# Three groups of heads on the first batch, conditioning of the second batch over nine units, one weight group loaded twice, and a new order of the last blocks

## The reference, cut to what matters

```python
def cond(r, k, v, w, u, temb):          # forward and backward decaying scans along T
    tf = sigmoid(sum(temb)); decay = exp(-exp(w)) * (0.5 + 0.5*tf)
    ek = exp(min(k, 30)); ekv = ek * v
    nf, df = scan(ekv), scan(ek)        # a = a*decay + x
    nb, db = scan_reverse(ekv), scan_reverse(ek)
    euk = exp(min(u + k, 30))
    return sigmoid(r) * (nf+nb-ekv+euk*v) / max(df+db-ek+euk, 1e-8) * (0.8+0.2*tf)
x = x + attention(cond(x, fside, fside, w1, u1, temb))   # 16 causal heads, W_K/Q/V/O
y = cond(x, fside, fside, w2, u2, temb)
x = x + sum_of_top2_of_8_experts(y) # each expert 256x256 plus bias, softmaxed gates
```

## Time and profile before

| | |
|---|---|
| median of 3 runs | 381.71 us (381.62 to 381.79) |
| the profiled execution | 381.94 us |
| its span | 380.1 us |
| TensorE busy | 351.5 us, 92% of the span |
| VectorE busy | 317.6 us, 84% |
| ScalarE busy | 255.8 us, 67% |
| GpSimd busy | 212.3 us, 56% |
| mean granted TensorE clock | 0.982 of full |

### The profile page before, as it was taken

How to read it: one execution, slowest core, us unless ns; L and a number is a source line. 1 busy time by engine, 2 the same in 40 slices (tenths; PEclk the granted TensorE clock), 3 DMA queues, 4 the chain that set the end, 5 groups by cost and what they waited for, 6 DMA issues and landing times.

```text
span 380.1 us, 7412 instructions
## 1 busy us (share of the span) xinstructions
PE 351.5 (92%) x2404; PEld 323.6 (85%) x2404; DVE 317.6 (84%) x883; ACT 255.8 (67%) x685; POOL 212.3 (56%) x223
## 2 busy tenths in 40 slices
PE   0897789999999999999999999999999998798997
PEld 0686679999999999899999999999999886685785
DVE  4979899999898988999899989998676747476576
ACT  5678888788778878877987889787877643210100
POOL 1865677864647669767857966886744341210000
PEclk9998899999999999999999999999999999898999
DMA  5660130100000000130100041000000000000000
GB/s 170 243 252 3 55 112 0 58 3 0 2 0 3 2 0 2 55 114 2 55 2 1 3 166 57 3 1 2 0 3 2 1 0 2 0 29 1 28 29 28
DMA packets 4597, 14.12 MB, mean 37 GB/s; under 512 B 840, under 2 KB 1872, under 8 KB 3920
## 3 DMA queue, kind: packets, MB, share of 16 engines
q1 hardware_dynamic: 4336, 13.65, 10.6%
q10 hardware_dynamic: 224, 0.01, 0.0%
HBM read 12.60 MB, written 1.05 MB: 36 GB/s over the span
## 4 chain that ended last, share of the span: by engine, by line
PE 67%; DVE 25%; issue 4%; ACT 3%; DMA 1%; DVEq 0%; ACTq 0%
PE psQK L900 7%; PE psQK L902 7%; PE psQK L901 7%; PE psT L970 4%; PE psO L900 4%; DVE tiles L703 3%; PE psO L902 3%; PE psO L901 3%; PE psS L900 3%; PE psS L901 3%; PE psS L902 3%; PE psV L900 3%; PE psS L956 3%; PE psZ L983 3%; PE psV L902 3%
## 5 line engine op out<-in xcount | busy, mean ns | idle before, releaser
L313 POOL TENSOR_SCALAR prob<-prob,rsum 128x256 f32<-128x256 f32 x60 | 55.7, 928 | 62.2 <-DVE rsum L738 62.2
L900 PE MATMUL psQK<-y_hi,w_hi 128*128 128x256 f32 x256 | 73.1, 286 | 1.2 <-DVE y_lo L653 1.2
L902 PE MATMUL psQK<-y_hi,w_lo 128*128 128x256 f32 x256 | 73.0, 285 | 0.0
L901 PE MATMUL psQK<-y_lo,w_hi 128*128 128x256 f32 x256 | 73.0, 285 | 0.0
L496 ACT ACTIVATE prob<-prob,ntop 128x256 f32<-128x256 f32 (+1 forms) x128 | 57.2, 449 | 23.3 <-DVE ntop L730 23.1
L319 POOL TENSOR_TENSOR z_lo<-z_lo,z_two 128x256 fp32r<-128x256 f32 x64 | 47.9, 748 | 36.0 <-DVE z_lo L756 36.0
L278 POOL TENSOR_TENSOR w_lo<-raw,w_hi 128x512 fp32r<-128x512 f32 x40 | 53.6, 1352 | 12.1 <-ACT w_hi L372 12.1
L900 PEld LDWEIGHTS psQK<-y_hi,w_hi 128*128 128x128 f32 x256 | 49.4, 193 | 3.1 <-issue 1.6
L901 PEld LDWEIGHTS psQK<-y_lo,w_hi 128*128 128x128 f32 x256 | 49.5, 194 | 1.3
L902 PEld LDWEIGHTS psQK<-y_hi,w_lo 128*128 128x128 f32 x256 | 49.5, 194 | 0.0
L742 DVE TENSOR_TENSOR qk<-psQK,qk 128x512 fp32r<-128x512 f32 x64 | 43.2, 676 | 6.0 <-ACT qk L484 6.0
(11 more groups left out here) (159 smaller groups left out, 1041.8 us busy)
## 6 DMA issues: line engine op xcount, KB each, us to landing
raw<-in_weights SPq DMA_DIRECT2D x5, 1024.0 KB, 5.2
raw<-in_weights SPq DMA_DIRECT2D x10, 512.0 KB, 4.2
out<-fT SPq DMA_DIRECT2D x8, 128.0 KB, 1.7
fT<-in_fT SPq DMA_DIRECT2D x2, 256.0 KB, 5.0
xT<-in_xT SPq DMA_DIRECT2D x2, 256.0 KB, 6.7
fT<-in_fT SPq DMA_DIRECT2D x1, 512.0 KB, 6.1
xT<-in_xT SPq DMA_DIRECT2D x1, 512.0 KB, 6.0
temb<-in_temb ACTq DMA_DIRECT2D x1, 1.0 KB, 3.4
```

What stands on the lines that cost most here:

```text
L313: pool.tensor_scalar(prob[:, k, P:3 * P], prob[:, k, P:3 * P], rsum[:, k, 1:2], None, ALU.mult).then_inc(shared, 1)
L900: pe.matmul(out, ah, bh, start=first and k == 0, stop=False)
L901: pe.matmul(out, ah, bl, start=False, stop=False)
L902: ins = pe.matmul(out, al, bh, start=False, stop=last and k == n - 1)
```

## The change

The order of the blocks: the first batch takes groups 0, 1 and 2, and the later batches go through what is loaded; group 0 is dropped from the weights early and loaded once more as load 3, so there are six loads (SOURCE gives the group of a load, SET the set it goes to). Number 1 of the conditioning takes the same places as the others, beginning at unit 1, so that y_low comes in iteration 9; the others begin at 9, 17, 25, 33, 40, 47 in place of 5, 13, 21, 29, 37, 45. In block 0 project_v stands behind project_qk, on all three engines. REFILL has new places. The order behind the loop is new on TensorE, VectorE and ScalarE; values(61) goes into the last unit.

```diff
-BLOCKS = [(g, b) for b in range(B) for g in (0, 1)] + [(g, b) for g in (2, 3) for b in range(B)]
+SOURCE = (0, 1, 2, 0, 3, GROUPS)
+SET = (0, 1, 0, 0, 1, 0)
+EXPERTS = len(SOURCE) - 1
+BLOCKS = [(0, 0), (1, 0), (2, 0), (2, 1), (1, 1), (1, 2), (2, 2), (2, 3), (1, 3), (3, 1), (3, 2), (3, 3)] + [(4, b) for b in range(B)]
...
+FREED_BY = (None, None, LAST_BLOCK[0], LAST_BLOCK[2], LAST_BLOCK[1], LAST_BLOCK[3])
...
-COND_START = (None, None, 5, 13, 21, 29, 37, 45)
+COND_START = (None, 1, 9, 17, 25, 33, 40, 47)
...
-DVE_FIRST = {"xd": (0, "M"), "xn": (0, "E"), "gd": (1, "M"), "gn": (1, "E"), "den": (2, "M"), "r0": (2, "E"), "r1": (3, "M"), "y": (4, "M")}
-POOL_FIRST = {"ekv": 0, "clamp": 1, "den": 2, "eukv": 3, "num": 4, "y_low": 5}
...
-REFILL = {1: (("qk", 0, -1), ("qk", 1, 0), ("v", 0, 1), ("qk", 2, 2), ("v", 1, 2), ("qk", 3, 3), ("o", 0, 5), ("o", 1, 8)),
-          2: (("qk", 0, 25), ("qk", 1, 26), ("v", 0, 26), ("qk", 2, 27), ("v", 1, 27), ("qk", 3, 29), ("o", 0, 33), ("o", 1, 34)),
-          3: (("qk", 0, 34), ("qk", 1, 35), ("qk", 2, 37), ("qk", 3, 40), ("v", 0, 41), ("v", 1, 42), ("o", 0, 43), ("o", 1, 45)),
-          4: (("v", 0, 48), ("v", 1, 49), ("qk", 0, 50), ("qk", 1, 51), ("qk", 2, 52), ("qk", 3, 53), ("o", 0, 54), ("o", 1, 55))}
+REFILL = {1: (("qk", 0, -1), ("qk", 1, 0), ("qk", 2, 1), ("qk", 3, 2), ("v", 0, 2), ("v", 1, 3), ("o", 0, 4), ("o", 1, 9)),
+          2: (("qk", 0, 5), ("qk", 1, 6), ("v", 0, 6), ("qk", 2, 7), ("v", 1, 7), ("qk", 3, 8), ("o", 0, 11), ("o", 1, 12)),
+          3: (("qk", 0, 30), ("qk", 1, 31), ("qk", 2, 32), ("qk", 3, 33), ("v", 0, 33), ("v", 1, 34), ("o", 0, 37), ("o", 1, 38)),
+          4: (("qk", 0, 36), ("qk", 1, 38), ("v", 0, 39), ("qk", 2, 40), ("v", 1, 41), ("qk", 3, 42), ("o", 0, 43), ("o", 1, 44)),
+          5: (("v", 0, 47), ("v", 1, 48), ("qk", 0, 49), ("qk", 1, 50), ("qk", 2, 51), ("qk", 3, 52), ("o", 0, 53), ("o", 1, 54))}
...
 # SyncE
-        for g in range(2, GROUPS + 1):
+        for g in range(2, EXPERTS):
+            load_qk(g)
             load_v(g)
-            load_qk(g)
             load_o(g)
+        load_v(EXPERTS)
+        load_qk(EXPERTS)
+        load_o(EXPERTS)
...
 # ScalarE, behind the loop
+        pT_high(UNITS - 2)
         z_high(UNITS - 3)
-        pT_high(UNITS - 2)
         gate_exp(1)
+        pT_high(UNITS - 1)
         tanh(2)
         z_high(UNITS - 2)
-        pT_high(UNITS - 1)
         z_high(UNITS - 1)
         y2_high(2)
         gates_copy(1)
         tanh(3)
         base_copy(1)
+        y2_high(3)
         gate_exp(2)
-        y2_high(3)
         gates_copy(2)
+        gate_exp(3)
         base_copy(2)
-        gate_exp(3)
         gates_copy(3)
         base_copy(3)
...
 # VectorE, loop (the same move on ScalarE and TensorE)
-            if 1 <= h <= TT:
+            if 1 <= h <= TT and i > 0:
                 v_low(i, h - 1)
             if u + 2 < UNITS:
                 qk_low(u + 2)
+            if 1 <= h <= TT and i == 0:
+                v_low(i, h - 1)
...
 # VectorE, behind the loop
+        pT_low(UNITS - 2)
         z_low(UNITS - 3)
-        pT_low(UNITS - 2)
         gate_first(1)
         add_experts(1)
         add_output(14)
+        add_experts(2)
+        pT_low(UNITS - 1)
+        gate_last(1)
         z_low(UNITS - 2)
-        pT_low(UNITS - 1)
-        add_experts(2)
-        gate_last(1)
         y2_last(2)
+        add_experts(3)
         z_low(UNITS - 1)
-        add_experts(3)
-        add_experts(4)
+        for j in range(4, 7):
+            add_experts(j)
         add_output(15)
-        add_experts(5)
+        y2_last(3)
         gate_first(2)
-        add_experts(6)
-        y2_last(3)
-        gate_last(2)
         add_experts(7)
         add_experts(8)
+        gate_last(2)
+        add_experts(9)
+        add_experts(10)
         gate_first(3)
-        add_experts(9)
+        add_experts(11)
         gate_last(3)
...
 # TensorE, the end
             if u >= UNITS - 2:
+                if u == UNITS - 1:
+                    values(UNITS - 3)
                 experts(u - UNITS + 3)
-        values(UNITS - 3)
+        output(len(BLOCKS) - 2, 1)
+        turn(UNITS - 1)
         experts(3)
-        turn(UNITS - 1)
-        output(len(BLOCKS) - 2, 1)
         values(UNITS - 2)
         experts(4)
         values(UNITS - 1)
         experts(5)
+        gates_turn(1)
+        experts(6)
         for c in range(CB):
             output(len(BLOCKS) - 1, c)
-        gates_turn(1)
         base(1)
-        experts(6)
-        logits(2)
-        late = {8: [(logits, 3)], 10: [(gates_turn, 2)], 12: [(base, 2)], 14: [(gates_turn, 3)], 16: [(base, 3)]}
+        late = {7: [(logits, 2)], 10: [(logits, 3)], 11: [(gates_turn, 2)], 13: [(base, 2)], 15: [(gates_turn, 3)], 17: [(base, 3)]}
```

More of the change, by code:

```diff
@@ L42 @@
 EXP_LIMIT = 10686474581524.463
-BLOCKS = [(g, b) for b in range(B) for g in (0, 1)] + [(g, b) for g in (2, 3) for b in range(B)]
+SOURCE = (0, 1, 2, 0, 3, GROUPS)
+SET = (0, 1, 0, 0, 1, 0)
+EXPERTS = len(SOURCE) - 1
+BLOCKS = [(0, 0), (1, 0), (2, 0), (2, 1), (1, 1), (1, 2), (2, 2), (2, 3), (1, 3), (3, 1), (3, 2), (3, 3)] + [(4, b) for b in range(B)]
 UNITS = GH * len(BLOCKS)
-LAST_BLOCK = [max(i for i, (g, _) in enumerate(BLOCKS) if g == group) for group in range(GROUPS)]
+LAST_BLOCK = [max(i for i, (n, _) in enumerate(BLOCKS) if n == load) for load in range(EXPERTS)]
+FREED_BY = (None, None, LAST_BLOCK[0], LAST_BLOCK[2], LAST_BLOCK[1], LAST_BLOCK[3])
 CONDS = [(b, w) for w in (0, 1) for b in range(B)]
-COND_START = (None, None, 5, 13, 21, 29, 37, 45)
+COND_START = (None, 1, 9, 17, 25, 33, 40, 47)
 COND_DVE, COND_ACT, COND_POOL = (13, 13), (9, 7), (5, 5)
@@ L337, in _ @@
             pieces = products(n)
-            for name, u in (POOL_FIRST if n == 1 else POOL_PLACES).items():
+            for name, u in POOL_PLACES.items():
                 if name != "y_low" or CONDS[n][1] == 0:
-                    at(u if n == 1 else COND_START[n] + u, pieces[name])
+                    at(COND_START[n] + u, pieces[name])
         for g, places in REFILL.items():
@@ L526, in _ @@
             pieces = cond(n)
-            for name, (u, place) in (ACT_FIRST if n == 1 else ACT_PLACES).items():
-                if name not in ("e1", "yhi") or CONDS[n][1] == 0:
-                    at(u if n == 1 else COND_START[n] + u, place, pieces[name])
+            for name, (u, place) in ACT_PLACES.items():
+                if COND_START[n] + u >= 0 and (name not in ("e1", "yhi") or CONDS[n][1] == 0):
+                    at(COND_START[n] + u, place, pieces[name])
         for g, places in REFILL.items():
@@ L566, in _ @@
                 qk_high(u + 2)
+            if 1 <= h <= TT and i == 0:
+                v_high(i, h - 1)
             if u >= 3:
@@ L819, in _ @@
             pieces = cond(n)
-            for name, (u, place) in (DVE_FIRST if n == 1 else DVE_PLACES).items():
-                at(u if n == 1 else COND_START[n] + u, place, pieces[name])
+            for name, (u, place) in DVE_PLACES.items():
+                at(COND_START[n] + u, place, pieces[name])
         def late_rests():
@@ L919, in project_qk_half @@
                 ins = three(psQK[u % 2][:, j * T:(j + 1) * T],
-                            [(both(w_hi, w_lo, ALL, g % 2, slot, c, slice(h * DH, (h + 1) * DH)),
+                            [(both(w_hi, w_lo, ALL, SET[g], slot, c, slice(h * DH, (h + 1) * DH)),
                               both(y_hi, y_lo, ALL, b, c))], c == j == 0, c == j == CB - 1)
@@ L935, in project_v_half @@
             return three(psV[:], [(both(y_hi, y_lo, ALL, b, c, slice(t * P, (t + 1) * P)),
-                                   both(w_hi, w_lo, ALL, g % 2, SLOT_V, c))], c == 0, c == CB - 1)
+                                   both(w_hi, w_lo, ALL, SET[g], SLOT_V, c))], c == 0, c == CB - 1)
         def project_v(i, t):
@@ L993, in output @@
                 pe.wait_ge(x_added, i)
-            o_hi, o_lo = (t[:, g % 2, SLOT_O].rearrange("p c n -> p (c n)").rearrange("p (h n) -> p h n", h=GH) for t in (w_hi, w_lo))
+            o_hi, o_lo = (t[:, SET[g], SLOT_O].rearrange("p c n -> p (c n)").rearrange("p (h n) -> p h n", h=GH) for t in (w_hi, w_lo))
             three(psO[:, c * T:(c + 1) * T], [(both(o_hi, o_lo, ALL, h, slice(c * P, (c + 1) * P)),
@@ L1052, in expert_cols @@
             return three(out, [(both(y_hi, y_lo, ALL, b, c, slice(t * P, (t + 1) * P)),
-                                                both(w_hi, w_lo, ALL, GROUPS % 2, EXPERT_SLOTS[slot], c, cols)) for c in range(CB)])
+                                                both(w_hi, w_lo, ALL, SET[EXPERTS], EXPERT_SLOTS[slot], c, cols)) for c in range(CB)])
         def experts(j):
@@ L1093, in _ @@
                 project_qk(u + 2)
+            if 1 <= h <= TT and i == 0:
+                project_v(i, h - 1)
             if u >= 3:
```

23 lines of the change are left out of this document (11 added, 12 removed).

## The result

The changed kernel takes 388.28 us (387.80 to 389.41, 4 runs) against 381.75 us before: ratio 1.0176, 95% interval 1.0153 to 1.0198. The forecast was 377.8. Lines have moved: L278 of before is L284, L313 is L319, the scans L608 and L611 are L616 and L619, L319 is L325, L703 is L711, L742 is L750, L746 is L754, L751 is L759, L956 is L968.

What follows compares the result with a forecast made beforehand. The prediction took VectorE (with the chain through GpSimd) to bound the start, TensorE's work the middle, and queue order the end. 381.9 + 4.4 + 0.6 - 8.9 = 378.0 us profiled, median 377.8; range 371.5 to 382.5.

Steps and rivals of the forecast that it cites:

- The end: Behind the loop: the new order removes named waits and two clock falls, less 0.3 us of new wait; - 8.9 us.
- the five waits: TensorE's waits at 315.79, 320.66, 324.95, 330.33 and 349.03 in the end, each removed by a move; sum 5.85 us.
- The ring in units 6 to 9: Start: project_qk(8) to (11) wait for GpSimd's load 2 refills, which have no slack; unit 10 2.7 us later before the clock.
- its entry: Start: 5.0 us gained before unit 6, which begins at 46.2; GpSimd's first piece is ready at 51.7.
- the lower bound: Gain before unit 6: 3 us if ScalarE becomes the limit, as it must do refills for load 2 sooner.
- 12.1 us: GpSimd's work from z_low(0) at 39.3 to load 2's first piece: three z_last, two shares, three refills, den, eukv and num.
- The clock: Start: one fall behind TensorE's wait of 3.2 us, + 1.7 us; a second fall kept for the range.
- The step from a long wait to a fall: Start: a 2.83 us wait was followed by a fallen clock, so the 3.2 us wait will be; + 1.7 us.
- The middle: Eight more refills lengthen VectorE's scans, so TensorE waits more for v_low; + 0.6 us, bounds 0 and 2.
- VectorE becomes the limit in the middle: Rival: half of 10.8 us from eight refills falls on VectorE's scans or other two-input work; 382.6 us, chance 0.04.
- The sum: Whole kernel: start + 4.4, middle + 0.6, end - 8.9 us, against the profiled execution of 381.9: 378.0 us.

Runs made afterwards that it cites:

- new_end: The kernel before with only the changed kernel's order of the end (ScalarE, VectorE, TensorE behind the loop, values(61) in the last unit): 372.1 us, ratio 0.9776.
- phases: The changed kernel with the last two conditionings begun at units 41 and 49 in place of 40 and 47: 385.4 us, ratio 1.0132.
- no_second_load: The changed kernel without load 3, group 2 used in place of group 0 for batches 1 to 3, same number of matmuls: 385.1 us, ratio 1.0106.
- pool_small: The changed kernel with GpSimd's refills of loads 3, 4 and 5 cut to two columns of the last dimension: 383.4 us, ratio 1.0091.
- apart: phases with refills of loads 3 to 5 moved out of the iterations of xd and xn, some two to an iteration: 390.4 us, ratio 1.0276.
- both_back: The changed kernel without load 3 and with the last two conditionings begun at units 41 and 49: 382.2 us, ratio 1.0046.
- pt_first: The changed kernel, load 2's qk refills one unit sooner; in units 0 to 5 ScalarE's conditioning pieces and refills behind the next iteration's pT_high: 378.5 us.

## Why the prediction was wrong, step by step

**The end: right.** - 8.9 forecast, - 9.2 measured, and alone (new_end) 9.2 as well by its profile (8.6 by the medians). The sum over the five waits of the earlier trace rows and two falls of the clock came to 9.25. This was the part with a row for every term.

**The ring in units 6 to 9: right in mechanism, its entry wrong.** Its period was forecast within a microsecond each. The step that failed is "5.2 us leave the stretch before unit 6 ... I take 5.0 us: unit 6 begins at 51.15 - 5.0 = 46.2". It began at 50.98, and at 48.2 or 48.3 in five experiments with the same start, whose clock fell elsewhere: in phases, no_second_load and pool_small from 36 to 42 us, in apart and both_back only from 58 us on. So about 3 of the 5 were won, the lower bound given there and much for the reason given there: ScalarE's order holds the units up (pt_first), so VectorE's shorter work did not shorten the units as much. GpSimd came late too. Its first refill for project_qk(8) ended at 55.3, and the forecast had 51.7:

```profile
40.97 0.74 POOL L325 TENSOR_TENSOR z_lo<-z_lo,z_two 128x256 fp32r<-128x256 f32 x1 [2.18 <-DVE z_lo L764]
...
54.02 1.26 POOL L284 TENSOR_TENSOR w_lo<-raw,w_hi 128x512 fp32r<-128x512 f32 x1
```

The pieces between are those of the sum and take its 12.1 us, but they started 1.6 us later than forecast, and GpSimd waited 2.5 us for VectorE among them, where the sum had 0.3.

**The clock: one fall forecast, two seen, one of them long.** The window from 40 to 60 us is at 0.74, so 5.2 us of work at the full level are missing, three times the 1.7 that the sum had. That isn't 5.2 us of time, since TensorE waits in this stretch anyway. apart and both_back have the same start with just one fall of 1.7 us, behind unit 6, as forecast, and their unit 10 begins at 76.9 and 77.0. The forecast was 74.6. So some 2.3 of the 2.9 us that the start missed are the entry, and about 0.6 the clock. The step from a long wait to a fall ("A wait of 2.83 us was followed by a fallen clock, so the wait of 3.2 will be") does not hold in the other traces: in new_end the same wait of 2.83 us is followed by a full clock, and so is the first wait for w_lo in apart, 2.81 us. That one fall did come behind the first wait for w_lo here, at 56 us, is luck. The stretches of the changed kernel at the lower level (0.50 is 1.2 GHz of 2.4), windows of 2 us, columns as in the earlier trace rows:

```profile
42.00:44.00 2.00, 0.38 (x2) 0.72 0.02 8
44.00:46.00 2.00, 2.00 (x10) 0.50 0.41 96
46.00:48.00 2.00, 2.00 (x6) 0.50 0.46 166
48.00:50.00 2.00, 2.00 (x12) 0.57 0.00 0
...
56.00:58.00 2.00, 2.00 (x13) 0.63 0.00 0
58.00:60.00 2.00, 2.00 (x10) 0.51 0.00 0
```

**The middle: the step that decided.** "TensorE's waits for v_low in the whole middle are 1.0 us before, with 16 refills there; I take + 0.6 for half as many more, bounds 0 and 2." It cost 8.3. The count is wrong to begin with: by REFILL, loads 2 to 4 have 24 pieces in the middle before, and the trace has 25 refills there and 27 after the change. Scaling by count would have given next to nothing. Three things were missed.

First, VectorE had no room for anything more: it was busy 19.45 of 20 us from 60 us on the earlier trace rows, and 18.9 to 19.8 from 180 to 260 us. The 1.0 us of the earlier trace rows was what was left after VectorE's slack had swallowed the rest of the refills' cost, and such a leftover can't be scaled. Taking load 3's refills out made VectorE busy 5.3 us less in the middle (216.4), where the rival started from 10.8 for eight refills, and gave back 3.7 us of time (no_second_load). The rival "VectorE becomes the limit in the middle" (382.6, chance 0.04) was this one, with 5.4 us, and I argued it down with that same row.

Second, 2.6 us from starting conditionings 7 units apart (phases): the diff shows 33, 40, 47 and the places of the pieces run to 7, and I only checked that all were ready in time, not that two now share an iteration.

Third, the 5.2 us of VectorE that leave the stretch before unit 6 don't leave the kernel: conditionings 2 to 5 each begin four units later, and six scans, about 5 us of VectorE, crossed into the middle. The sum has no term for them. What they cost in time was not separated.

Of the 8.3 us, 2.6 are still there in both_back. Against the kernel before, units 11, 14 and 18 are 1.6 us longer, where the last refills of loads 1 and 2 stand beside conditioning number 2, and units 42, 43, 50, 51 and 55 are 3.4 longer; units 30, 31, 38, 39, 46 and 47, which the kernel before had over the steady length, are 2.4 shorter. What causes these was not tried.

**The sum.** 4.4 + 0.6 - 8.9 = - 3.9 forecast; 7.3 + 8.3 - 9.2 = + 6.4 measured. With the middle at its measured size alone the forecast would have been + 3.8: the sign turned there.

## What to carry to other kernels

Split a change by stages and run the stage that gains by itself: here a reordered end was worth 9.2 us and was buried under 15.6 us of losses elsewhere. A piece of weights that is made in the same unit in which it is needed closes a ring through every engine; one unit of slack cost nothing and gave 8.2 us. When an engine off the top of the list is 97% busy in a stage, don't scale the small wait that is seen there: list what the change puts on that engine in the stage, with work that only moves in from another stage, count the pieces in the listing and in the trace, and look whether periodic pieces that are moved closer together meet in one iteration.

## What the runs showed of the hardware

With 24 GpSimd refills of about 1.3 us cut, VectorE's product with thalf took 742 ns in place of 1441, a backward scan 852 in place of 990 and a forward scan 724 in place of 842, on average (pool_small against the changed kernel). With ScalarE's refills cut in their place, as many, the time didn't change by more than its interval. A pair of scans, forward or backward, took 1.26 us at its shortest, and a backward pair 3.44 us beside two refills (apart). In the changed kernel the granted clock was 0.50 to 0.63 for about 4 us behind a wait of TensorE of 2.12 us, and 0.50 to 0.57 from 44 to 50 us, behind one of 1.77 us. In apart and both_back, with the same start, no fall followed the same wait (1.76 and 1.77 us). In new_end a wait of 2.83 us at 31.61 was followed by a clock of 1.00, in the kernel before the same wait at 31.75 by 0.50.
